# Softmax cross attention of the last decoder layer: one two-bank unit of maxima per chunk read by ScalarE, and the order of the two score products

## The reference, cut to what matters

```
q = split_heads(Q @ Wq.T + bq)            # 16 heads, 8 features, 1024 queries
k = split_heads(K @ Wk.T + bk)            # 6404 keys
v = split_heads(V @ Wv.T + bv)
scores = einsum('bhqd,bhkd->bhqk', q, k) / sqrt(8)
scores = where(mask == 0, -1e9, scores)
attn   = softmax(scores, axis=-1)
ctx    = einsum('bhqk,bhkd->bhqd', attn, v)
return ctx_with_heads_side_by_side @ Wo.T + bo
```

## Time and profile before

| | us |
|---|---|
| time, median of 3 executions | 5749.84 (5748.77 to 5754.9) |
| the profiled execution: time | 5753.69 |
| the profiled execution: span of the trace | 5752.0 |
| maxima only, turns 0 to 13 | 4391 to 4496 |
| maxima and scores together, turns 14 to 103 | 4496 to 5431 |
| scores only | 5431 to 5540 |
| PE busy over the whole span | 5158.6 |
| VectorE busy | 3192.3 |
| ScalarE busy | 3458.9 |

### The profile page before, as it was taken

One profiled execution on the slowest core, in us unless ns is written; L12 is line 12 of the kernel. 1 busy time (PEld: TensorE's weight loads), 2 busy tenths in 40 slices (PEclk: granted clock), 3 DMA queues, 4 the chain that ended last, 5 costly groups with the idle time before them and its releaser, 6 DMA issues. The chain is left out here.

```text
span 5752.0 us, 67092 instructions
## 1 busy us (share of the span) xinstructions
PE 5158.6 (90%) x26382; PEld 1644.9 (29%) x26382; DVE 3192.3 (56%) x3563; ACT 3458.9 (60%) x3537; POOL 2226.0 (39%) x1118
## 2 busy tenths in 40 slices
PE   8879999999999999889897799998886788888889
PEld 3323333333333333233343311111332111111123
DVE  5687777777777772225522300000257988888723
ACT  4566666666666666511122499999125677777861
POOL 1139899998989899716352000000000000000000
PEclk7889999999999999899998799999895899999999
DMA  1000000000000000000000300000203000000010
GB/s 51 15 1 1 5 1 5 1 5 1 4 5 1 5 1 5 21 22 1 2 0 10 111 22 21 13 10 5 79 25 136 3 11 12 12 14 10 6 46 31
DMA packets 67590, 104.45 MB, mean 18 GB/s; under 512 B 12100, under 2 KB 52134, under 8 KB 65164
## 3 DMA queue, kind: packets, MB, share of 16 engines
q1 hardware_dynamic: 67070, 99.34, 5.2%
q10 hardware_dynamic: 206, 0.83, 0.0%
HBM read 74.58 MB, written 25.43 MB: 17 GB/s over the span
## 5 line engine op out<-in xcount | busy, mean ns | idle before, releaser
L2518 ACT ACTIVATE Pr<-ps,key_bias 128x1024 f32<-128x1024 f32 x816 | 864.6, 1110 | 658.9 <-PE ps L2383 658.8
L2619 DVE TENSOR_REDUCE red<-ps 128x2 f32<-128x1024 f32 (+1 forms) x767 | 904.3, 1180 | 422.9 <-PE ps L2370 422.0
L2720 POOL TENSOR_TENSOR Ps<-Ps,Pr 128x1024 f32<-128x1024 f32 x400 | 943.0, 2358 | 145.0 <-ACT Pr L2518 144.2
L2729 POOL TENSOR_TENSOR Ps<-Ps,Pr 128x1024 f32<-128x1024 f32 x400 | 941.2, 2353 | 0.0
L3354 DVE TENSOR_REDUCE red<-ps 128x1 f32<-128x512 f32 (+3 forms) x1024 | 877.3, 907 | 95.8 <-PE ps L3227 76.0
L3310 ACT ACTIVATE Pr<-ps 128x1024 f32<-128x1024 f32 x816 | 786.2, 1021 | 228.3 <-PE ps L3237 227.4
L2383 PE MATMUL ps<-Q,Kr 64*128 64x512 f32 x3264 | 805.2, 610 | 43.6 <-DVE ps L2343 24.8
L2403 PE MATMUL ps<-Pr,Vc 128*64 128x512 f32 x3264 | 790.1, 605 | 0.0
L3484 ACT ACTIVATE Pr<-ps 128x2048 f32<-128x2048 f32 x467 | 726.2, 2034 | 1.6 <-PE ps L3447 1.6
L2343 DVE CAST ps<-seeds 128x1024 f32<-128x1024 bf16 x499 | 601.1, 1221 | 187.5 <-ACT Pr L2518 172.5
L3227 PE MATMUL ps<-Kp,Q 52*128 52x512 bf16 (+1 forms) x1664 | 442.7, 412 | 171.1 <-DVE red L3354 125.2
(11 more groups left out here) (583 smaller groups left out, 5068.2 us busy)
## 6 DMA issues: line engine op xcount, KB each, us to landing
L_dram_K<-parts SPq DMA_DIRECT2D x26, 384.0 KB, 3.0
Kp<-L_dram_K SPq DMA_DIRECT2D x14, 624.0 KB
L_dram_K<-parts SPq DMA_DIRECT2D x26, 256.0 KB, 2.9
wB<-L_ffn_shares SPq DMA_DIRECT2D x1, 6144.0 KB
w<-L_ffn_experts_w_dram SPq DMA_DIRECT2D x24, 256.0 KB
Kp<-L_dram_K SPq DMA_DIRECT2D x14, 416.0 KB
over<-cross_dram_inverse SPq DMA_DIRECT2D x14, 256.0 KB, 3.8
wB<-L_ffn_shares SPq DMA_DIRECT2D x1, 3584.0 KB, 12.7
```

Source lines behind the costliest of these rows:

```text
L2518: nc.scalar.activation(Pr[:, t % 4, half].rearrange("p a n -> p (a n)"), ps[:, 2 * half:2 * half + 2, :].rearrange("p a n -> p (a n)"), AC ...
L2619: nc.vector.tensor_reduce(red[:, i // C % 2, q, :, i % C], ps[:, b:b + 2, 0:ctx.keys_in(i % C)], AX, ALU.max).then_inc(*reduced.up())
L2720: nc.gpsimd.tensor_tensor(into, into, src, ALU.add).then_inc(*summed0.up())
L2729: nc.gpsimd.tensor_tensor(into, into, src, ALU.add).then_inc(*summed1.up())
```

## The change

Three things. In each chunk from turn 14 on one unit of two banks (unit 6 or unit 3, by the same parity) is no longer reduced from PSUM by VectorE. ScalarE copies it to SBUF as fp32 (`put_aside`), and VectorE then takes the maximum of each bank from there with a `tensor_scalar` that writes its own accumulator (`reduce_aside`), behind the reduction of the unit three numbers later. Its bank is free when the copy ends. The counts of `reduced` are adapted. And the two score products of a half are issued with the head first that the last maxima matmul did not use.

```diff
+    beside = k.tile(stack, "beside", [128, 2, 2, HALF])
...
+    def aside_unit(i):
+        return 6 if (i - LAG) % 2 == 0 else 3
+    def aside_number(i):
+        return i - LAG
+    def reduced_number(i, u):
+        n = unit_number(i, u) - act_number(i, u)
+        return n if i < LAG else n - aside_number(i) - (u > aside_unit(i))
     def taken_off(i, u):
-        n = act_number(i, u)
-        return copied.at(n + 1) if u in act_units(i) else reduced.at(unit_number(i, u) - n + 1)
+        if i >= LAG and u == aside_unit(i):
+            return aside.at(aside_number(i) + 1)
+        return copied.at(act_number(i, u) + 1) if u in act_units(i) else reduced.at(reduced_number(i, u) + 1)
...
     def pe():
         taken = {0: None, 2: None, 4: None, 7: None}
+        last_head = [1]
...
                 q, a = item // 2, item % 2
+                last_head[0] = a
...
-            for a in range(2):
+            for a in (1 - last_head[0], last_head[0]):
                 mm = nc.tensor.matmul(ps[:, 2 * half + a, :], lhsT=Kp[head(a), p % 3, kt * 128:(kt + 1) * 128], rhs=Q[head(a), p, HALVES[half]], start=True, stop=True)
...
+        def put_aside(g, u):
+            first, n, b = units(g)[u]
+            m, keys = aside_number(g), ctx.keys_in(g % C)
+            nc.scalar.wait_ge(*maxima_mm.at(unit_number(g, u) + 1))
+            if m >= 2:
+                nc.scalar.wait_ge(*aside_reduced.at(2 * (m - 1)))
+            nc.scalar.copy(beside[:, m % 2, :, 0:keys], ps[:, b:b + n, 0:keys]).then_inc(*aside.up())
...
                     for u in ours:
                         if min(items.index(u), 1) == half:
                             bring(g, u)
+                    if LAG <= g < N and aside_unit(g) in items and items.index(aside_unit(g)) == half:
+                        put_aside(g, aside_unit(g))
...
+                if LAG <= g < N and aside_unit(g) in items[2:]:
+                    put_aside(g, aside_unit(g))
...
+        def reduce_aside(g):
+            first, n, b = units(g)[aside_unit(g)]
+            m, keys = aside_number(g), ctx.keys_in(g % C)
+            nc.vector.wait_ge(*aside.at(m + 1))
+            for a in range(n):
+                nc.vector.tensor_scalar(beside[:, m % 2, a, 0:keys], beside[:, m % 2, a, 0:keys], -3e38, -3e38, ALU.max, ALU.max,
+                                        accum_out=red[:, g // C % 2, first + a, g % C:g % C + 1]).then_inc(*aside_reduced.up())
...
+                if g >= LAG and u == aside_unit(g):
+                    continue
                 nc.vector.wait_ge(*maxima_mm.at(unit_number(g, u) + 1))
...
+                if g >= LAG and u == aside_unit(g) + 3:
+                    reduce_aside(g)
...
-                nc.vector.wait_ge(*reduced.at(unit_number(g + 1, 0) - act_number(g + 1, 0)))
+                nc.vector.wait_ge(*reduced.at(reduced_number(g + 1, 0)))
+                if p:
+                    nc.vector.wait_ge(*aside_reduced.at(2 * aside_number(g + 1)))
```

More of the change, by code:

```diff
@@ L3131, in small_softmax @@
         "out_copied", "out_stored0", "out_stored1", "zeroed")
+    aside, aside_reduced = k("scores_aside", "aside_reduced")
     out_stored = (out_stored0, out_stored1)
```

## The result

The changed kernel took 5830.53 us (median of 4, 5822.61 to 5833.71) against 5752.37 us (median of 4): ratio 1.0135, 95% interval 1.0122 to 1.0147, 78 us slower. The forecast was 5805, with a range of 5760 to 5855. Its profiled execution took 5822.61 us, with a span of 5820.9.

What follows compares the result with a forecast made beforehand. It took a PE-VectorE chain through PSUM banks, 20.34 us per two chunks, as the bound. Added 0.35 + 0.36 + 0.76 = 1.47 us, times 35.5 pairs 52, plus 3, gave +55 on 5749.84: 5805, range 5760 to 5855.

Steps and rivals of the forecast that it cites:

- the chain: Per step: first unit's matmul, its reduction, third unit's matmul on the freed bank, products; closes two chunks at 20.34 us.
- What the change removes: Units 6 and 3, each second in its step, leave VectorE's queue but lie off the waiting path: gain 0.
- Term 1: ScalarE's copy between a step's two exponentials delays the matmul of unit 8 or 5: 0.35 us per two chunks.
- A: The chunk with units of 2, 1, 2, ... banks, where unit 6 is copied; forecast 0.18 us late at unit 8.
- Terms 2 and 3: Compares queued on VectorE behind unit 9 in one chunk, unit 6 in the next: losses 0.36 and 0.76 us.
- The slacks of 0.54 and 0.14 us: Time each chunk's two compares can take before delaying PE: 0.54 us behind unit 9, 0.14 behind unit 6.
- a: VectorE time of a chunk's two compares together: forecast 0.9 us, 0.45 apiece, bounds 0.68 and 1.58.
- the second rival: VectorE's compares run at one element a cycle, 0.60 + 0.075 us each, 1.35 a pair: 5837 us; chance 0.30.
- The order of the score products: PE's new head order spares 0.21 us slots, at best 22 us if PE were the bound; taken as 0.
- The first rival: VectorE's load is the bound, so each chunk saves 0.24 us, 17 us in all: 5733 us; chance 0.12.
- The third: Compares fall into VectorE's idle time and only the copies cost, 12 us: 5762 us; chance 0.08.

Runs made afterwards that it cites:

- the ring: The kernel before, with one-bank units only from turn 14 on, going round banks 4, 5 and 7: 5726.17 us, ratio 0.9958.

## Why the prediction was right

**What bounds the kernel.** Shown. Where the order of a step's work on PE was the old one and the clock full, the chain gives each measured period, from 19.73 to 22.39 us, to about 0.1 us, once a compare has its measured price; and lowering VectorE's work (no compares) or raising it (the ring) moved the time the other way than load would.

**What the change removes: nothing on the path.** Shown by the run without compares.

**Term 1, the copies.** Forecast 0.35 us per two chunks, measured 0.30 (0.16 late in A by the rows above).

**Terms 2 and 3, the compares' place.** The slacks of 0.54 and 0.14 us were right: with the measured a = 1.21 they make 0.67 + 1.07, with the copies 2.04, against 2.06 measured. The periods at a = 0.67 and 1.21, and PE's starts at 1.21 and 2.42, follow the same forms.

**The size of a.** This is the term that was mis-sized, and behind it a mechanism: what forecast and measurement differ by is the second rival. I took 0.9 from the 480 ns of a TENSOR_SCALAR without accumulator; it was 1.21. The compare is as slow as a one-bank reduction, as that rival has it, but cheaper than its 1.35, since the readout of 82 ns hides. That puts the result, +78, between the forecast's +55 and the rival's +87. 2.06 x 35.5 is 73; I had put 3 for the short chunks, and where exactly the remaining 5 lie no run shows. The number alone would not have decided it: the range took in both prices, and it is the row of 678 ns that tells them apart.

The Trainium skill, "PSUM — Partial Sum Buffer" (Specifications (TRN2)), lists tensor_scalar "without an accumulator output" among the instructions that send two elements at a time. It says so of 2-byte elements written to PSUM, not of fp32 in SBUF, so it was a hint and not the rule itself; here the same shape took 678 ns with that output and 418 without it. I should have given the hint the larger chance.

**The order of the score products: 0.** Shown twice.

**The first rival** (VectorE is the bound) would have needed the run without compares to be faster. **The third** (compares hide where they stand) failed too, though what it describes happens one place further on.

Not settled: what the three-step turns and the 260-key chunks add. The run with the compares in gaps is some 15 us slower than before while 0.31 x 35.5 explains 11. In the profiled executions the seven stretches from one writing of the maxima rows into `Q` to the next (ScalarE's CAST, 4488 to 5436 us before) take 947.6 us in the kernel before, 954.8 without compares and 961.8 with the compares in gaps: some 1 us more for each pair of heads than without compares, though a full chunk pays 0.01. The compares of a pair's last chunk, which stand ahead of its rows, are the likely place; that was not tested.

## What to carry to other kernels

An engine that is 97% busy in a steady pattern need not be the bound: compare the distances between its starts with the smallest distance that the same instruction shows elsewhere, and follow one bank through its matmul, reader and next matmul. Take from an engine the instruction that the chain goes through, since any other gains nothing here, and put work that was deferred where the engine idles, not at the next convenient place in program order; the same four compares cost 1.76 us of a period or 0.01. Before splitting a group of matmuls, look whether they run beside each other.

## What the runs showed of the hardware

- A fp32 tensor_scalar of 128x512 in SBUF takes 418 ns, with an accumulator output 678, as much as a one-bank reduction from PSUM (684). The readout of 82 ns does not delay the next instruction: starts stay 0.60 us apart.
- Four fp32 matmuls of 9 output partitions each over 512 columns, at partitions 0, 32, 64 and 96, take 0.97 us together until PE's next matmul, and two of them 0.96.
- With waits of 2.25 and 1.72 us on PE in two chunks the granted clock fell to 1.2 GHz twice in 27.27 us, 0.88 on average, which took 2.45 us of each period. At full clock the longer part of the period was measured (15.34), the shorter one (9.47) is the changed kernel's 8.26 and 1.21.
